# One-hot marks of places moved from VectorE to ScalarE in six edge passes of a graph network

## Chip, cores and metric
One core of a Trainium2 chip runs the whole program in one launch. The metric is device time in microseconds, from the start to the end of the execution; lower is better.

## What is computed
Four graph layers run one after the other over 6250 nodes with 256 features and 100000 edges, each followed by a residual and a layer norm:

```
x = layernorm(x + L0(x)); x = layernorm(x + L1(x)); x = layernorm(x + L2(x)); x = layernorm(x + L3(x))
# L0: two GAT layers, 4 heads of 64 and 1 head of 64
alpha = segment_softmax(leaky_relu(al_s[src] + al_d[dst]), dst)
out   = segment_sum(h[src] * alpha, dst)
# L1: two heads of 128
e   = exp(-leaky_relu(s_l[src] + s_r[dst]))
out = elu(segment_sum(e * h[dst], src) / segment_sum(e, src))
# L2: 8 heads of 32
s   = sum(q[row] * k[col])
out = segment_sum(segment_softmax(s, row) * v[col], row)
# L3: two graph convolutions, 128 and 64 wide, with batch norm
out = segment_sum(h[src] * dinv[src] * dinv[dst], dst)
```

In each of these the edges gather a row of a table of nodes and are summed by their target node. That makes six passes over the edges: a1e and a2e (L0), be (L1), te (L2), g1e and g2e (L3).

## The kernel before
The edges are first sorted twice, by source and by target. After that every node window of 128 nodes has its edges in groups of 128 slots; 832 groups (NSLOT) make 104 batches (NBT) of 8 groups. Of each slot `order.row` holds the row to gather, `order.place` the place of its target node in the window (0 to 127, larger for an empty slot), and `order.window` the group's window. The tables and sums stay in float32.

A pass goes over the 104 batches, written out in full (`batches`), each engine with its own `step`, tied by semaphores:

- POOL (`gather`, L948 and L1325) issues 8 indirect DMAs a batch. It waits for DVE's copy of the index of the batch and for the ring of row buffers to be free: in the attention passes until DVE has weighed the batch that lay there (`s_summand`), in the sum passes until PE has summed it. The ring holds 4 batches, in te 2.
- DVE `mark` (L1109 to L1113, L1354 to L1358) makes `onehot`: for 8 groups of 128 slots a 128x1024 float32 tile that is 1 where the lane number equals the slot's place. There are two buffers, so it waits for PE's sums of the batch before last.
- DVE `weigh` multiplies the gathered rows by their weights into `summand`, two groups at a time, `add` adds PE's result of a group to its window in `acc`, with a window number held in a register. The registers are loaded for a few batches at a time (`Windows.load`).
- PE `sums` (L987) multiplies `onehot` by `summand`, one matmul a group into one of four PSUM banks; `add` must have freed the bank. In the sum passes (L1339) PE takes the gathered rows as they are, and has eight banks.
- In the passes with a guarded softmax (a1e, a2e, te) there is a running maximum besides: PE `flat` turns the logits, DVE `scan_forward` and `scan_back` scan them, PE `ends` brings the edges of the scan to one row, DVE scans that row (`row_scan_forward`, `row_scan_back`, `drop`), PE `columns` (L1012) spreads it again, using row 0 of `onehot`, DVE `widen` and `top` finish the maximum, PE `back` turns it back and DVE `subtract` makes the argument of the exponent.
- ACT does little: `fading` (L1083) takes the exponential that PE's `columns` makes ready, with which DVE `fade_first` scales an open window; `weights` (L1075) takes the exponentials of the arguments into `summand`. In be it has only `weights`; in the sum passes there is no ACT block.

The order of DVE's work in a batch is written out in `step` (L1231 and L1364). There the mark stands behind the last adds of the batch before last and in front of the third weighing and the forward scan; in the sum passes it is the first thing of a step. PE's order is in L1029: flat, sums 2 and 3, ends, sums 4 and 5, columns, sum 6, back, sum 7, with small differences between the passes.

Of the kernel before, what the change touches and what calls it, by code (L numbers as in the profile page):

```python
# [13 lines left out]
P = 128  # L14
# [49 lines left out]
def bc(ap, shape):  # L64
    return ap.to_broadcast(shape)
# [767 lines left out]
def attention_pass(nc, c, stage, order, tables, table, width, acc, Y, H, C, kind, node=None, value_c0=0, queries=None, early=None):  # L833
# [21 lines left out]
    with ExitStack() as stack:  # L855
# [5 lines left out]
        place_row = [m.sb(f"place_row{b}", [P, 8 * P], F16) for b in range(2)]  # L861
        turned = [m.sb(f"turned{b}", [P, 8 * P], F32 if dot else BF16) for b in range(2)]
        onehot = [m.sb(f"onehot{b}", [P, 8, P]) for b in range(2)]
        argument = [m.sb(f"argument{b}", [P, NARG, H, 8]) for b in range(2)]
        ps_u = [m.ps(f"ps_u{b}", [P, 512]) for b in range(4)]
        if dot:
# [6 lines left out]
        if guarded:  # L873
# [15 lines left out]
        s_flags = [m.sem(f"flags{b}") for b in range(2)]  # L889
        (s_index, s_turned, s_onehot, s_at_node, s_spread, s_raw, s_logit, s_joined, s_product, s_query, s_weight, s_summand, s_summed, s_added,  # L890
         s_flat, s_forward, s_local, s_ends, s_row_forward, s_row_peak, s_fall, s_columns, s_fade, s_widened, s_peak, s_back, s_argument, s_own,
         s_faded, s_ready, s_early, s_passed, s_passed_pe, s_passed_sp, s_passed_act) = (m.sem(x) for x in (
            "index", "turned", "onehot", "at_node", "spread", "raw", "logit", "joined", "product", "query", "weight", "summand", "summed", "added",
            "flat", "forward", "local", "ends", "row_forward", "row_peak", "fall", "columns", "fade", "widened", "peak", "back", "argument", "own",
            "faded", "ready", "early", "passed", "passed_pe", "passed_sp", "passed_act"))

        def lives(t):
            return not isinstance(t, int) or 0 <= t < NBT
# [8 lines left out]
        def batches(eng, step, last=NBT, windows=None):  # L907


            for t in range(last):  # L910
                if windows is not None and t % U == 0:
                    windows.load(t)
                step(t, t % U)

        with nc.Block() as block:
# [157 lines left out]
            @block.scalar  # L1073
            def _(act):
                def weights(t, b):  # L1075
                    act.wait_ge(s_argument, t + 1)
                    wait(act, s_summed, t * 8 - 8)
                    out = summand[:, b, :, :].rearrange("p k (h n) -> p h k n", h=H)
                    act.activation(out[:, :, :, C], argument[b][:, 0, :, :], ACT.Exp, scale=1.0 if guarded else -1.0).then_inc(s_weight, 1)
                    if gat:  # L1080
                        act.activation(out[:, :, :, C + 1], argument[b][:, 1, :, :], ACT.Exp).then_inc(s_weight, 1)

                def fading(t, b):  # L1083
                    act.wait_ge(s_columns, t + 1)
                    wait(act, s_faded, t - 1)
                    act.activation(fade[b][:, :], ps_l[:, 256:256 + H], ACT.Exp).then_inc(s_fade, 1)

                def step(t, j):
                    if guarded:
                        fading(t, j % 2)  # L1090
                    weights(t, j % 2)

                batches(act, step)

            @block.vector
            def _(dve):
# [6 lines left out]
                def turn(t, b):  # L1103
                    if lives(t):
                        dve.wait_ge(s_place[b], t * 8 + (16 - b * 8))
                        wait(dve, s_query if dot else s_at_node, t * 4 - 4 if dot else t - 1)
                        dve.tensor_scalar(turned[b][:, :], place_row[b][:, :], c.lane_p[:, :], None, ALU.is_equal).then_inc(s_turned, 1)  # L1107

                def mark(t, b):  # L1109
                    if lives(t):  # L1110
                        wait(dve, s_summed, t * 8 - 8)
                        dve.tensor_tensor(onehot[b][:, :, :], bc(c.lane[:, :].rearrange("p (k n) -> p k n", k=1), [P, 8, P]),
                                          bc(order.place[:, bass.ds(t * 8, 8)].rearrange("p (k n) -> p k n", n=1), [P, 8, P]), ALU.is_equal).then_inc(s_onehot, 1)  # L1113

                def weigh(t, b, r, pair):
                    if not lives(t):
# [114 lines left out]
                def step(t, j):  # L1231
# [18 lines left out]
                    else:  # L1250
# [8 lines left out]
                        if gat:  # L1259
                            join(t, b)  # L1260
                        add(t - 2, 7, -9, j)
                    mark(t, b)
                    weigh(t - 1, n, rp, 2)
                    if guarded:
                        scan_forward(t, b)
# [33 lines left out]
def sum_pass(nc, c, stage, order, table, width, acc):  # L1299
# [4 lines left out]
    with ExitStack() as stack:  # L1304
        m = Memory(nc, stack, stage)
        rows = m.sb("rows", [P, RING, 8, width])
        index = m.sb("index", [P, RING, 8], I32)
        onehot = [m.sb(f"onehot{b}", [P, 8, P]) for b in range(2)]
        ps_u = [m.ps(f"ps_u{b}", [P, 512]) for b in range(8)]
        s_rows = [[m.sem(f"rows{r}_{h}") for h in range(2)] for r in range(RING)]  # L1310
        s_index, s_onehot, s_summed, s_added, s_passed = (m.sem(x) for x in ("index", "onehot", "summed", "added", "passed"))

        def lives(t):
            return not isinstance(t, int) or 0 <= t < NBT
# [7 lines left out]
        with nc.Block() as block:  # L1322
# [15 lines left out]
            def _(pe):  # L1338
# [8 lines left out]

                batches(pe, step)

            @block.vector  # L1350
            def _(dve):
                windows = Windows(nc, order, mybir.EngineType.DVE, -8, RING)

                def mark(t, b):  # L1354
                    if lives(t):
                        wait(dve, s_summed, t * 8 - 8)
                        dve.tensor_tensor(onehot[b][:, :, :], bc(c.lane[:, :].rearrange("p (k n) -> p k n", k=1), [P, 8, P]),
                                          bc(order.place[:, bass.ds(t * 8, 8)].rearrange("p (k n) -> p k n", n=1), [P, 8, P]), ALU.is_equal).then_inc(s_onehot, 1)  # L1358
# [553 lines left out]
```

## Time and profile before

| | us |
|---|---|
| median of 3 runs | 13213.7 (13208.91 to 13229.04) |
| profiled execution | 13124.58 |
| its span, first to last instruction | 13122.8 |
| DVE busy | 8087.8 (62%) |
| PE busy | 7310.8 (56%) |
| POOL busy | 5296.6 (40%) |
| ACT busy | 580.3 (4%) |

The profile is of one execution. "Busy" is the time in which an engine works on an instruction; waits, register and issue instructions are not in it. A line such as L1112 is a line of the kernel. In a row with a bracket, the bracket tells how long the engine was idle before the instruction and what ended the wait; "issue" is a wait for nothing that the profile shows, "remote" one whose releaser it can't tell. PEld is the load of weights into TensorE. The sorting takes the first 2700 us or so, and holds none of the changed code.

### The profile page before, as it was taken

The page shows a single profiled execution, that of the slowest core. Times are in us where ns is not written, and L with a number is a line of the kernel's source. Part 1 is how long each engine was busy: PE and PEld are TensorE (multiplying, and loading weights), DVE is VectorE, ACT ScalarE, POOL GpSimd, SP SyncE. Part 2 cuts the span into 40 slices and gives each one's busy share as a digit, 9 for nine tenths or more (in the row PEclk, how much of TensorE's full clock was granted, in tenths as well). Part 3 has the DMA queues.
Part 4 walks back from the last instruction along what each step waited for, and adds up shares of the span by engine and source line. Part 5 has one row for each costly group of instructions (what it writes and reads, how often), then busy time and mean ns, then how long its engine had stood idle before and what let it go on. Part 6 is the DMA issues. An engine that isn't in the chain of part 4 may idle for free. (4 is left out here: it accounts for less than half of the span.)

```text
span 13122.8 us, 152037 instructions
## 1 busy us (share of the span) xinstructions
PE 7310.8 (56%) x32826; PEld 4771.1 (36%) x32826; DVE 8087.8 (62%) x27204; ACT 580.3 (4%) x2200; POOL 5296.6 (40%) x5059
## 2 busy tenths in 40 slices
PE   4555355568886455556665466666666433333335
PEld 2333233344444344433333234444443323223333
DVE  9999899957777444445665666666664322332224
ACT  0000000010001000001000100000001000000001
POOL 0000000046662566615777033333330666556670
PEclk6777677765655555557666776666665555555557
DMA  0111111133332221213444133333330111211111
GB/s 18 50 50 51 38 50 50 53 93 107 106 106 53 60 43 42 42 10 105 114 111 110 64 113 112 112 112 111 111 102 31 45 45 45 38 20 23 23 23 22
DMA packets 456540, 857.24 MB, mean 65 GB/s; under 512 B 136865, under 2 KB 197974, under 8 KB 455766
## 3 DMA queue, kind: packets, MB, share of 16 engines
q0 software_dynamic: 226304, 550.69, 17.4%
q1 hardware_dynamic: 229718, 300.70, 7.8%
q8 instruction: 196, 3.21, 0.1%
q14 instruction: 322, 2.64, 0.1%
HBM read 798.81 MB, written 52.14 MB: 65 GB/s over the span
## 5 line engine op out<-in xcount | busy, mean ns | idle before, releaser
L954 POOL DMA_INDIRECT all_Y<-table,te_index x832 | 851.1, 1023 | 1384.9 <-DVE all_Y L1123 1177.1
L954 POOL DMA_INDIRECT all_Y<-table,a1e_index x832 | 891.3, 1071 | 454.6 <-issue 245.4
L954 POOL DMA_INDIRECT all_Y<-table,be_index x832 | 942.0, 1132 | 292.9 <-issue 245.8
L954 POOL DMA_INDIRECT all_Y<-table,a2e_index x832 | 833.0, 1001 | 515.5 <-DVE all_Y L1123 293.1
L1330 POOL DMA_INDIRECT g2e_rows<-table,g2e_index x832 | 839.6, 1009 | 447.1 <-issue 247.8
L1330 POOL DMA_INDIRECT g1e_rows<-table,g1e_index x832 | 815.4, 980 | 481.5 <-issue 236.0
L994 PE MATMUL te_ps_u<-all_Y,te_onehot 128*128 128x264 f32 x1664 | 749.1, 566 | 458.1 <-DVE all_Y L1123 384.2
L1123 DVE TENSOR_TENSOR all_Y<-all_Y 128x512 f32<-128x512 f32 (+1 forms) x1664 | 964.6, 580 | 40.3 <-issue 18.1
L994 PE MATMUL be_ps_u<-all_Y,be_onehot 128*128 128x258 f32 x1664 | 722.7, 572 | 430.0 <-DVE all_acc L1135 257.5
L994 PE MATMUL a1e_ps_u<-all_Y,a1e_onehot 128*128 128x264 f32 x1664 | 878.8, 654 | 83.8 <-DVE all_acc L1135 47.2
L1346 PE MATMUL g1e_ps_u<-g1e_rows,g1e_onehot 128*128 128x128 f32 x1664 | 485.1, 444 | 757.8 <-issue 478.3
L1346 PE MATMUL g2e_ps_u<-g2e_rows,g2e_onehot 128*128 128x64 f32 x1664 | 426.0, 429 | 798.4 <-issue 412.6
L940 POOL MEMSET all_acc<- 128x13200 f32 (+2 forms) x4 | 35.9, 8973 | 1903.0 <-POOLq L80 1794.4
L1371 DVE TENSOR_TENSOR all_acc<-all_acc,g1e_ps_u 128x128 f32 x832 | 239.4, 288 | 828.7 <-DMA te_turns<-turns_src 501.6
L1371 DVE TENSOR_TENSOR all_acc<-all_acc,g2e_ps_u 128x64 f32 x832 | 184.0, 221 | 862.6 <-DMA te_turns<-turns_src 414.5
L1346 PEld LDWEIGHTS g1e_ps_u<-g1e_rows,g1e_onehot 128*128 128x128 f32 x1664 | 378.6, 291 | 864.2 <-issue 658.9
L493 DVE TENSOR_SCALAR all_acc<-all_Y,all_acc 128x832 f16<-128x832 f16 x1568 | 687.4, 438 | 0.0
L1346 PEld LDWEIGHTS g2e_ps_u<-g2e_rows,g2e_onehot 128*128 128x128 f32 x1664 | 377.1, 324 | 847.3 <-issue 555.1
L994 PEld LDWEIGHTS be_ps_u<-all_Y,be_onehot 128*128 128x128 f32 x1664 | 383.0, 267 | 711.9 <-issue 500.2
L994 PEld LDWEIGHTS te_ps_u<-all_Y,te_onehot 128*128 128x128 f32 x1664 | 372.9, 257 | 668.1 <-DVE all_Y L1123 627.7
L983 PE MATMUL te_ps_q<-all_X,te_turned 128*128 x1664 | 570.7, 503 | 23.2 <-DVE te_turned L1107 22.1
L994 PE MATMUL a2e_ps_u<-all_Y,a2e_onehot 128*128 128x66 f32 x1664 | 498.8, 429 | 90.6 <-DVE all_acc L1135 69.8
(464 smaller groups left out, 15600.2 us busy)
## 6 DMA issues: line engine op xcount, KB each, us to landing
all_Y<-lows SPq DMA_DIRECT2D x196, 256.0 KB
all_Y<-codes SPq DMA_DIRECT2D x196, 256.0 KB
a1e_place_row<-places_dst SPq DMA_DIRECT2D x104, 256.0 KB
a2e_place_row<-places_dst SPq DMA_DIRECT2D x104, 256.0 KB
be_place_row<-places_src SPq DMA_DIRECT2D x104, 256.0 KB
te_place_row<-places_src SPq DMA_DIRECT2D x104, 256.0 KB
all_Y<-table,a1e_index POOLq DMA_INDIRECT x832
all_Y<-table,a2e_index POOLq DMA_INDIRECT x832
```

What stands on the lines that cost most here:

```text
L493: dve.tensor_scalar(column1[b][:, k, :], lane16, column[b][:, k:k + 1], None, ALU.is_equal)
L940: pool.memset(acc[:, 0:NW * R], 0.0).then_inc(s_ready, 1)
L954: pool.indirect_dma_start(out=rows[:, r, k, :], out_offset=None, in_=table, in_offset=bass.IndirectOffsetOnAxis(ap=index[:, r, k:k + 1], a ...
L983: last = pe.matmul(ps_q[pair % 2][:, j * HC:(j + 1) * HC], turned[b][:, k * P:(k + 1) * P], queries[:, bass.ds(windows.at(windows_j, chunk ...
L994: pe.matmul(ps_u[k % 4][:, 0:R], onehot[b][:, k, :], summand[:, b, k, :], start=True, stop=True).then_inc(s_summed, 1)
L1123: dve.tensor_tensor(out[:, :, :, 0:C], rows[:, r, ks, value_c0:value_c0 + HC].rearrange("p k (h n) -> p k h n", h=H), bc(out[:, :, :, C:C ...
L1330: pool.indirect_dma_start(out=rows[:, r, k, :], out_offset=None, in_=table, in_offset=bass.IndirectOffsetOnAxis(ap=index[:, r, k:k + 1], a ...
L1346: pe.matmul(ps_u[k][:, 0:width], onehot[b][:, k, :], rows[:, r, k, :], start=True, stop=True).then_inc(s_summed, 1)
L1371: dve.tensor_tensor(mine, mine, ps_u[k][:, 0:width], ALU.add).then_inc(s_added, 1)
```

## The change
ScalarE makes `onehot` in all six passes. Places and lane numbers are whole numbers, so 1 - |place - lane|, cut at zero, is 1 where they agree and 0 elsewhere. ScalarE takes the distance of each of the 8 groups in an ACTIVATE of its own (Abs, with the place as the bias of a partition) into a float16 tile, then Relu of one minus the distance for the 8 at once. In the attention passes `mark(0, 0)` comes first, and the mark of batch t+1 behind the weights of batch t; in the sum passes ScalarE gets a block that makes one mark after the other. DVE's `mark` goes in both functions. One tile `distance` is added, and one semaphore.

```diff
@@ attention_pass
+        distance = m.sb("distance", [P, 8, P], F16)
...
             @block.scalar
...
+                def mark(t, b):
+                    if lives(t):
+                        wait(act, s_onehot, t)
+                        for k in range(8):
+                            act.activation(distance[:, k, :], c.lane[:, :], ACT.Abs, scale=-1.0, bias=order.place[:, t * 8 + k:t * 8 + k + 1]).then_inc(s_distance, 1)
+                        act.wait_ge(s_distance, t * 8 + 8)
+                        wait(act, s_summed, t * 8 - 8)
+                        act.activation(onehot[b][:, :, :], distance[:, :, :], ACT.Relu, scale=-1.0, bias=1.0).then_inc(s_onehot, 1)
...
                     weights(t, j % 2)
-
+                    mark(t + 1, 1 - j % 2)
+
+                mark(0, 0)
                 batches(act, step)
...
             @block.vector
...
-                def mark(t, b):
-                    if lives(t):
-                        wait(dve, s_summed, t * 8 - 8)
-                        dve.tensor_tensor(onehot[b][:, :, :], bc(c.lane[:, :].rearrange("p (k n) -> p k n", k=1), [P, 8, P]),
-                                          bc(order.place[:, bass.ds(t * 8, 8)].rearrange("p (k n) -> p k n", n=1), [P, 8, P]), ALU.is_equal).then_inc(s_onehot, 1)
...
-                    mark(t, b)
                     weigh(t - 1, n, rp, 2)
@@ sum_pass
+            @block.scalar
+            def _(act):
+                def mark(t, b):
...
+                for t in range(NBT):
+                    mark(t, t % 2)
+
             @block.vector
...
-                    mark(t, r % 2)
                     for k in range(8):
```

The `mark` of the sum passes' ScalarE block is the same five lines as above, and DVE's `mark` (L1354) goes there as it does in the attention passes.

## Rows read from the trace of the kernel before

**Rows 1.** The page, part 1: busy time of each engine, share, instructions.
```profile
PE 7310.8 (56%) x32826; PEld 4771.1 (36%) x32826; DVE 8087.8 (62%) x27204; ACT 580.3 (4%) x2200; POOL 5296.6 (40%) x5059
```

**Rows 2.** Stretches: us, then PE, PEld, DVE, ACT, POOL busy (count), PEclk, DMA share, GB/s.
```profile
2760.00:4110.00 1350.00, 1085.07 (x3884) 642.38 (x3885) 1039.16 (x2964) 56.73 (x308) 871.41 (x813) 0.59 0.41 104
...
6020.00:7240.00 1220.00, 766.59 (x2416) 437.64 (x2416) 751.94 (x1813) 23.43 (x101) 928.38 (x819) 0.66 0.43 111
7600.00:9820.00 2220.00, 1469.07 (x4701) 953.69 (x4701) 1511.66 (x3269) 51.04 (x206) 835.41 (x816) 0.69 0.40 111
10205.00:11420.00 1215.00, 478.81 (x1640) 373.14 (x1640) 355.55 (x1018) 0.00 (x0) 804.10 (x823) 0.54 0.19 45
11605.00:12790.00 1185.00, 417.40 (x1630) 369.15 (x1629) 301.79 (x1018) 0.00 (x0) 824.49 (x819) 0.50 0.14 23
```

**Rows 3.** Groups by form, DVE: the mark in te; the other five alike, 126.7 to 127.1.
```profile
L1112 DVE TENSOR_TENSOR te_onehot<-all_lane,all_place 128x1024 f32<-128x1024 f32 x104 | 126.7, 1218 | 0.1
```

**Rows 4.** The page, part 5: gathers of a1e, be, g2e, g1e; busy, mean ns, idle.
```profile
L954 POOL DMA_INDIRECT all_Y<-table,a1e_index x832 | 891.3, 1071 | 454.6 <-issue 245.4
L954 POOL DMA_INDIRECT all_Y<-table,be_index x832 | 942.0, 1132 | 292.9 <-issue 245.8
...
L1330 POOL DMA_INDIRECT g2e_rows<-table,g2e_index x832 | 839.6, 1009 | 447.1 <-issue 247.8
L1330 POOL DMA_INDIRECT g1e_rows<-table,g1e_index x832 | 815.4, 980 | 481.5 <-issue 236.0
```

**Rows 5.** Timeline of te around one mark: start, duration, engine, line.
```profile
7914.59 0.27 PE L1001 MATMUL te_ps_l<-all_ident,te_joined 128*72 128x128 f32 x1
7915.03 1.22 DVE L1112 TENSOR_TENSOR te_onehot<-all_lane,all_place 128x1024 f32<-128x1024 f32 x1
...
7916.16 0.69 DVE L1123 TENSOR_TENSOR all_Y<-all_Y 128x512 f32<-128x512 f32 x1
...
7918.16 0.64 PE L1009 MATMUL te_ps_r<-all_ident,te_local 72*1 72x72 f32 x4 [3.30 <-DVE te_local L1193]
```

**Rows 6.** Timeline of a1e: PE's sums 2 and 3 and its ends matmul.
```profile
3407.98 2.08 PE L994 MATMUL a1e_ps_u<-all_Y,a1e_onehot 128*128 128x264 f32 x4
...
3411.04 0.29 PE L1009 MATMUL a1e_ps_r<-all_ident,a1e_local 36*1 36x36 f32 x4 [0.98 <-DVE a1e_local L1193]
```

**Rows 7.** Waits in the stretches of rows 2 (a2e: 4330 to 5650): us, times, longest.
```profile
DVE a2e_forward L1188 <- remote: 324.9, 47, 9.4
...
DVE a1e_forward L1188 <- remote: 23.7, 1, 23.7
...
POOL g1e_rows L1330 <- PE g1e_ps_u L1346: 172.7, 79, 8.6
```

**Rows 8.** Timeline of be: two gathers on POOL, then DVE's mark beside the second.
```profile
6512.32 0.95 POOL L954 DMA_INDIRECT all_Y<-table,be_index  x1 [0.30 <-issue]
6513.57 1.57 POOL L954 DMA_INDIRECT all_Y<-table,be_index  x1 [0.30 <-issue]
...
6513.10 1.22 DVE L1112 TENSOR_TENSOR be_onehot<-all_lane,all_place 128x1024 f32<-128x1024 f32 x1
```

**Rows 9.** Timeline of g1e: a late and a quick add on DVE, POOL's gather after standstill.
```profile
10747.32 0.29 DVE L1371 TENSOR_TENSOR all_acc<-all_acc,g1e_ps_u 128x128 f32 x1 [5.31 <-DMA te_turns<-turns_src]
...
10752.53 0.29 DVE L1371 TENSOR_TENSOR all_acc<-all_acc,g1e_ps_u 128x128 f32 x1 [0.21 <-DVE all_acc L1371]
...
10751.40 1.04 POOL L1330 DMA_INDIRECT g1e_rows<-table,g1e_index  x1 [5.12 <-PE g1e_ps_u L1346]
```

**Rows 10.** ACT: four ACTIVATEs in a row; one group; the table load; a1e's fading.
```profile
12900.11 0.76 ACT L734 ACTIVATE gfl_turned<-gfl_ps_t 128x128 f32<-128x128 f32 x4 [2.45 <-PE gfl_ps_t L697]
...
L1589 ACT ACTIVATE a1l_tile<-a1l_ps_o 128x264 f32<-128x264 f32 x50 | 19.6, 391 | 28.8 <-PE a1l_ps_o L708 28.8
...
L237 ACT ACT_TABLE_LOAD x1 | 1.3, 1283 | 4.8 <-PEq L109 4.8
...
3414.40 0.17 ACT L1086 ACTIVATE a1e_fade<-a1e_ps_l 128x4 f32<-128x4 f32 x1 [9.76 <-PE a1e_ps_l L1019]
```

More of the change, by code:

```diff
@@ L891, in attention_pass @@
          s_flat, s_forward, s_local, s_ends, s_row_forward, s_row_peak, s_fall, s_columns, s_fade, s_widened, s_peak, s_back, s_argument, s_own,
-         s_faded, s_ready, s_early, s_passed, s_passed_pe, s_passed_sp, s_passed_act) = (m.sem(x) for x in (
+         s_faded, s_ready, s_early, s_distance, s_passed, s_passed_pe, s_passed_sp, s_passed_act) = (m.sem(x) for x in (
             "index", "turned", "onehot", "at_node", "spread", "raw", "logit", "joined", "product", "query", "weight", "summand", "summed", "added",
             "flat", "forward", "local", "ends", "row_forward", "row_peak", "fall", "columns", "fade", "widened", "peak", "back", "argument", "own",
-            "faded", "ready", "early", "passed", "passed_pe", "passed_sp", "passed_act"))
+            "faded", "ready", "early", "distance", "passed", "passed_pe", "passed_sp", "passed_act"))
         def lives(t):
@@ L1308, in sum_pass @@
         onehot = [m.sb(f"onehot{b}", [P, 8, P]) for b in range(2)]
+        distance = m.sb("distance", [P, 8, P], F16)
         ps_u = [m.ps(f"ps_u{b}", [P, 512]) for b in range(8)]
         s_rows = [[m.sem(f"rows{r}_{h}") for h in range(2)] for r in range(RING)]
-        s_index, s_onehot, s_summed, s_added, s_passed = (m.sem(x) for x in ("index", "onehot", "summed", "added", "passed"))
+        s_index, s_onehot, s_summed, s_added, s_distance, s_passed = (m.sem(x) for x in ("index", "onehot", "summed", "added", "distance", "passed"))
         def lives(t):
@@ L1348, in _ @@
                 batches(pe, step)
+            @block.scalar
+            def _(act):
+                def mark(t, b):
+                    if lives(t):
+                        wait(act, s_onehot, t)
+                        for k in range(8):
+                            act.activation(distance[:, k, :], c.lane[:, :], ACT.Abs, scale=-1.0, bias=order.place[:, t * 8 + k:t * 8 + k + 1]).then_inc(s_distance, 1)
+                        act.wait_ge(s_distance, t * 8 + 8)
+                        wait(act, s_summed, t * 8 - 8)
+                        act.activation(onehot[b][:, :, :], distance[:, :, :], ACT.Relu, scale=-1.0, bias=1.0).then_inc(s_onehot, 1)
+                for t in range(NBT):
+                    mark(t, t % 2)
             @block.vector
@@ L1352, in _ @@
                 windows = Windows(nc, order, mybir.EngineType.DVE, -8, RING)
[L1354 to L1358, printed above, removed]
                 def stage_index(t, r):
```

## The prediction, made before the changed kernel ran
> **What bounds the kernel now.** I read the page's busy shares first: no engine is full over the span, DVE 62%, PE 56%, POOL 40%, ACT 4% [rows 1]. So the stages have different limits, and the change touches six of them. The table of stretches gives each pass's middle: te 2220 us, a1e 1350, be 1220, g1e 1215, g2e 1185 [rows 2]; a2e is near a1e. ACT works 0 to 57 us in any of them, so it has room everywhere; what matters is whether DVE's 1.22 us mark [rows 3] lies on the path of each pass.
>
> - te: 2220 us for 816 gathers, that is 102 batches, 21.8 us each. DVE is busy 1512 us and idle only where PE or ACT answers it; POOL is busy 835 us [rows 2]. The timeline shows the mark between the turn and the weighing with no gap on either side [rows 5]. DVE sets the pace.
> - a1e: 1350 us, DVE 1039, POOL 871 [rows 2]. DVE is in one long chain with PE. POOL's gathers with their 0.3 us of issue between them need less: 891 busy + 245 of issue = 1137 us of some 1380 [rows 4].
> - a2e: 47 batches lose time in front of the forward scan, 324.9 us together, to a "remote" releaser; in a1e that happens once, 23.7 us [rows 7].
> - be: POOL is the limit. 942 us busy, and of its 292.9 us of idle 245.8 are issue, which leaves 47 for any wait [rows 4].
> - g1e and g2e: POOL runs 804 and 824 us in 1215 and 1185 [rows 2]; with issue 1054 and 1071. The rest, 161 and 114 us, is POOL waiting; in g1e 172.7 us are put down to PE's sums [rows 7]. DVE is busy for only 356 and 302 us, yet it is what POOL finally waits for: the adds stand 0.2 us apart at one time and over 5 us apart at another [rows 9]. The releaser named there is a DMA of a finished pass, so the true cause of the long gaps is not in the view. They appear while POOL gathers without a pause and end when POOL has stood still for 5 us. Some queue seems to fill under gap-free gathers, and PE's results reach DVE late. I take this as a limit that the mark does not touch.
>
> **The change, part by part.** Removed: 104 marks on DVE in each pass. On DVE a mark costs from its start to the next one's start: 7915.03 to 7916.16, 1.13 us [rows 5]; times 104 is 118 us a pass, 705 in six, if all of it were on the path.
>
> Added on ACT, per batch: eight distances of 128x128 and one Relu of 128x1024. Four ACTIVATEs of 128x128 took 0.76 us together, one alone 0.27 [rows 10]: 0.16 us each once they follow one another, so eight take 0.27 + 7 x 0.16 = 1.4 us (2.2 if nothing overlaps). The Relu: 264 elements took 0.391 us [rows 10], against 128 in 0.27 that is 0.85 to 0.9 ns an element, so 1024 take 1.05 us. A mark on ACT is 2.5 us, at most 3.3, against 11.5 to 22 us a batch. I cost it at nothing; its cover is ACT's idleness. Its order: behind the weights of batch t stands the mark of t+1, and behind that the fading of t+1. In a1e ACT stood idle 9.76 us between the weights and the fading [rows 10], room for 2.5. The mark's own wait is for the last sum of t-1, which PE issues around then; the mark is first needed by PE's columns, just before the fading. In be the next thing queued is the weights a batch later, in the sum passes nothing. There ACT has to keep up with DVE's quick step, eight adds 0.5 us apart and an index copy, 4.2 us [rows 9]; 2.5 to 3.3 does.
>
> The table of functions: the one load of the whole trace took 1.28 us and serves Exp, Copy and Square [rows 10]. No row shows Abs or Relu. From below it is nothing. From above two loads a batch, 2.6 us, still fit into ACT's gap, so I take nothing. The Trainium skill (ScalarE: Activation LUTs, Table sets) says that relu and abs are in every set; no run here shows it. Its rules for authors say to keep relu on VectorE since it is faster there per element; by that the work would be dearer, and the rows say that it is dearer on an engine that has nothing else to do.
>
> The port. A gather on POOL takes 0.95 us alone and 1.57 when a mark runs on DVE beside it [rows 8]. Over a pass the gathers spend more than 832 x 0.95 = 790 us by 101 in a1e, 152 in be, 25 in g1e, 49 in g2e [rows 4]. The mark's share is between nothing (the weighing next to it stretches gathers too) and 0.6 us x 104 = 64 us in be, and all of it in g1e and g2e. The Trainium skill (SBUF — State Buffer, Who interferes with whom) says that a tensor_tensor with two SBUF inputs contends only with POOL's reads and did not stall descriptor generation. By that rule the relief would be nil and be would gain at most its 47 us. The trace shows the stretching, so I count relief, but only part.
>
> Now the passes.
> - te: flat's transpose has ended at 7914.86, before the mark does, so the scan behind the weighing needn't wait, and PE's ends stand 3.3 us waiting for DVE's local [rows 5]. All of it, but for rounding: 117.
> - a1e: PE's four passes of sums end at 3410.06 and its ends matmul started at 3411.04 [rows 6], so 0.98 of 1.13 gets through at most where the clock is slow: 102 to 118 (104 batches). Bound from below 0, if late answers of PE come here too. I take 95.
> - a2e: where DVE waits at the scan the mark is hidden. That leaves 57 of 104 batches, x 1.13 = 64; more bursts may bring more waits. Bounds 0 and 118; I take 45.
> - be: 47 of waiting plus 64 of stretching are the upper end, 111; 0 the lower. POOL issues on either way; I take 45, nearer to the wait than to the sum.
> - g1e: the upper end is the mark, 118 (POOL has 177 + 25 to give); the lower 0, if the late answers set the pace. I take 35, somewhat over the port's 25.
> - g2e: 118 and 0 likewise, POOL having 115 + 49; 35.
>
> Sum: 117 + 95 + 45 + 45 + 35 + 35 = 372 us. The profiled execution took 13124.6 us, so it would take 12753. The median of the runs is 13213.7, 0.7% above the profiled one, though the runs lie within 0.15%; I take the gain off the median: 12842, say 12840. About 0.2% is what a measurement of this kernel can tell from no change.
>
> **Rivals.**
> A. Full release: the marks are on the path in all DVE-driven passes, and the long gaps in g1e and g2e shrink with DVE's load. Then te 118, a1e 118, a2e 64, be 111, g1e 118, g2e 118 = 647, and 12567. For it: in g1e's quick stretches an add comes every 0.5 us [rows 9], eight in 4.0, so the mark is a fifth of DVE's step. Against: the over-5 us gaps, which hold no DVE work. Chance 0.20.
> B. Gathers bind: be, g1e and g2e average 1.49, 1.48 and 1.45 us a gather (stretch over POOL's count) [rows 2], where an undisturbed one needs 1.25; if the unseen queue sets that average, all three give 15 together, a2e 15, te 117 and a1e 95: 242, and 12972. Chance 0.15.
> C. Slower: in a1e DVE's slowness gives POOL a pause each batch, and a1e has one remote wait before the forward scan where a2e has 47 [rows 7]. If the freed DVE makes gathers in a1e gap-free, that wait comes there too, at 324.9 / 47 = 6.9 us. The other passes gain 277, so it decides from 277 / 6.9 = 40 of 104 batches on. With 60 batches: 414 - 277 = 137 more, 13351. Against: a1e takes 13.3 us a batch now (813 gathers, 8 a batch), 12.2 after the change, and POOL needs 11.0 [rows 2], which leaves a pause, and POOL's standstill ends such a phase. Chance 0.07.
> D. No change: the time shows up again as waits for PE in every pass, since PE is also near its limit in te and a1e at a low clock. The idle PE before ends [rows 5] speaks against it. 13214, chance 0.04.
>
> **How the numbers follow.** The forecast has the other 0.54, and spans gains of 270 to 500. The range runs from 12610, most of the way to A, to 13000, past B: outside are C, D and the far part of A, under 2 in 10. Faster: forecast, A and B, 0.89. Same: 0.04. Slower: 0.07.
>
> **What the changed profile would show.** No onehot write on DVE in the passes and DVE busy down by about 760 us; on ACT 4992 distances near 0.27 us and 624 Relus near 1.05, so ACT up by some 2000 us of counted time, with one table load. te's middle near 2105 us. In te the forward scan follows weigh 2 without a gap: a gap there says that flat is late. The gathers near 0.95 us where marks stretched them. Wrong would be: more remote waits before a1e's scan (C), the fading waiting for ACT rather than PE's columns, more than two table loads, or g1e and g2e shorter by over 100 us each (A).

## The result: 0.7% slower, and the profile after

Ten timed runs each: 13290.65 us (13235.81 to 13305.5) with the change, 13211.89 (13123.92 to 13247.68) before; ratio 1.0067, 95% interval 1.0043 to 1.0091. The forecast was 12840, between 12610 and 13000. The profiled execution of after took 13302.03 us, that of before 13124.58, which is one of the quick ones of its kernel (two of the ten timed runs lie there too): the two profiles differ by 177 us, the medians by 79. The sum below is made between the profiles.

The page of after, part 1, as in [rows 1]:
```profile
PE 7158.1 (54%) x32826; PEld 4698.6 (35%) x32826; DVE 7399.3 (56%) x26580; ACT 2706.2 (20%) x7816; POOL 5028.2 (38%) x5059
```
The page of after, part 5, the gathers, as in [rows 4] (busy, mean ns of one | idle, what ended most of it):
```profile
L955 POOL DMA_INDIRECT all_Y<-table,te_index x832 | 852.7, 1025 | 1257.7 <-DVE all_Y L1129 1047.6
L955 POOL DMA_INDIRECT all_Y<-table,a1e_index x832 | 846.9, 1018 | 623.2 <-DVE all_Y L1129 397.3
L955 POOL DMA_INDIRECT all_Y<-table,a2e_index x832 | 801.3, 963 | 607.9 <-DVE all_Y L1129 370.9
L955 POOL DMA_INDIRECT all_Y<-table,be_index x832 | 830.0, 998 | 462.8 <-issue 239.9
L1336 POOL DMA_INDIRECT g2e_rows<-table,g2e_index x832 | 786.6, 945 | 530.8 <-issue 258.8
L1336 POOL DMA_INDIRECT g1e_rows<-table,g1e_index x832 | 786.6, 945 | 529.0 <-issue 262.4
```
In the attention passes busy and idle together are the time from the first gather to the last: in be 942.0 + 292.9 = 1235 before and 830.0 + 462.8 = 1293 after. The change made POOL 112 us shorter there and idle 170 us longer. In a1e it is busy 44 less and idle 169 more. In the sum passes the idle time also holds some 68 and 82 us ahead of the first gather. From the first gather to the last, us:

| | a1e | a2e | be | te | g1e | g2e |
|---|---|---|---|---|---|---|
| before | 1345 | 1347 | 1232 | 2235 | 1228 | 1203 |
| after | 1469 | 1408 | 1291 | 2109 | 1247 | 1234 |
| difference | +124 | +61 | +59 | -126 | +19 | +31 |

These make +168 of the 177. So te gained what was forecast, and the other five lost. Waits of DVE in after, in a1e, a2e and be (us, times, longest), as in [rows 7]:
```profile
DVE a1e_forward L1194 <- remote: 178.2, 29, 13.4
...
DVE a1e_widened L1219 <- remote: 80.8, 21, 11.8
...
DVE a1e_row_forward L1204 <- remote: 29.5, 8, 6.3
...
DVE a2e_widened L1219 <- remote: 388.1, 81, 6.8
...
DVE all_acc L1141 <- remote: 411.6, 88, 14.5
```
The same three kinds in a1e were 28.5 us before: a forward scan of 23.7, a widening of 4.8. In a2e the remote waits of DVE grew as well, from 431 us to 590 together; most stood before the forward scan (327.3 us) and now stand before the widening. The waits named remote stand in front of a different operation in each line, but each of these waits for a semaphore that PE raises: flat, columns, ends, sums. In be the wait before the adds was 139.3 us, 33 times, and is now 411.6 us, 88 times.

The timeline of after, g1e, shows what such a wait is, as in [rows 9] (start, duration, engine, line, in brackets the idle time and its releaser):
```profile
10800.27 0.29 DVE L1384 TENSOR_TENSOR all_acc<-all_acc,g1e_ps_u 128x128 f32 x1 [4.34 <-issue]
...
10801.58 0.95 POOL L1336 DMA_INDIRECT g1e_rows<-table,g1e_index  x1 [0.30 <-issue]
10802.83 0.94 POOL L1336 DMA_INDIRECT g1e_rows<-table,g1e_index  x1 [0.30 <-issue]
10804.08 0.95 POOL L1336 DMA_INDIRECT g1e_rows<-table,g1e_index  x1 [0.30 <-issue]
10805.19 0.29 DVE L1384 TENSOR_TENSOR all_acc<-all_acc,g1e_ps_u 128x128 f32 x1 [4.64 <-issue]
...
10805.53 0.80 PE L1352 MATMUL g1e_ps_u<-g1e_rows,g1e_onehot 128*128 128x128 f32 x2 [4.07 <-issue]
...
10810.32 0.95 POOL L1336 DMA_INDIRECT g1e_rows<-table,g1e_index  x1 [0.31 <-issue]
...
10814.95 1.06 ACT L1365 ACTIVATE g1e_onehot<-g1e_distance 128x1024 f32<-128x1024 f16 x1 [24.04 <-DMA te_turns<-turns_src]
10815.00 0.29 DVE L1384 TENSOR_TENSOR all_acc<-all_acc,g1e_ps_u 128x128 f32 x1 [3.91 <-DMA te_turns<-turns_src]
...
10816.27 0.94 POOL L1336 DMA_INDIRECT g1e_rows<-table,g1e_index  x1 [5.00 <-PE g1e_ps_u L1352]
10817.38 0.29 DVE L1384 TENSOR_TENSOR all_acc<-all_acc,g1e_ps_u 128x128 f32 x1 [2.01 <-issue]
...
10817.88 0.29 DVE L1384 TENSOR_TENSOR all_acc<-all_acc,g1e_ps_u 128x128 f32 x1 [0.21 <-DVE all_acc L1384]
10818.38 0.29 DVE L1384 TENSOR_TENSOR all_acc<-all_acc,g1e_ps_u 128x128 f32 x1 [0.21 <-DVE all_acc L1384]
```
Read it by the code. PE has eight banks, so the matmul at 10805.53 is the one that waited for the add at 10805.19 to free its bank; the seven sums ahead of it stand in the trace as done long ago (counted off, the add at 10810.80 takes one that started at 10788.6). The answer from DVE to PE is quick: the matmul starts 0.34 us after the add's start, 0.05 after its end. The answer from PE to DVE is late, and ACT's Relu, which waits for the same count of the same semaphore as the add at 10815.00, starts with it. Two engines see it at one time, so what is late is not the engine that waits. It lasts while POOL gathers every 1.25 us; when POOL has stood still for 5 us, the adds follow each other every 0.50 us. I call these the late answers. The profile's end of a matmul is modelled. The Trainium skill (Perfetto Trace Analysis, Tensor Engine Instruction) says the same, and that the update goes out only after PSUM has acknowledged the write.

Whether the sum or its update was late can't be told from the ends of the matmuls, but the trace also holds the times of the semaphores' updates (625 for the sums of 816 matmuls of this pass; the others are missing in it). Seven of them stand between 10815.62 and 10815.87, 0.04 us apart, while POOL stands still; no two recorded sums of this pass end less than 0.22 us apart. So these sums were done, and their updates were held back and came together. An update of DVE or ACT in this pass comes within 0.02 us of its instruction's end. Of PE's, 261 of the 625 come over 1.5 us behind the last recorded matmul that could have sent them.

### The profile page after: what moved, and what is told of

Read it like the earlier page. It is cut to its first block and busy times, and to the rows that moved or that the text cites. A ratio compares the mean times of both kernels' runs of the same rounds, so it can differ in the third digit from the quotient of the medians.

```text
span 13300.3 us, 157641 instructions
## 1 busy us (share of the span) xinstructions
PE 7158.1 (54%) x32826; PEld 4698.6 (35%) x32826; DVE 7399.3 (56%) x26580; ACT 2706.2 (20%) x7816; POOL 5028.2 (38%) x5059
## 5 line engine op out<-in xcount | busy, mean ns | idle before, releaser
L955 POOL DMA_INDIRECT all_Y<-table,a1e_index x832 | 846.9, 1018 | 623.2 <-DVE all_Y L1129 397.3
L955 POOL DMA_INDIRECT all_Y<-table,a2e_index x832 | 801.3, 963 | 607.9 <-DVE all_Y L1129 370.9
L955 POOL DMA_INDIRECT all_Y<-table,be_index x832 | 830.0, 998 | 462.8 <-issue 239.9
L1336 POOL DMA_INDIRECT g2e_rows<-table,g2e_index x832 | 786.6, 945 | 530.8 <-issue 258.8
L1336 POOL DMA_INDIRECT g1e_rows<-table,g1e_index x832 | 786.6, 945 | 529.0 <-issue 262.4
L995 PE MATMUL be_ps_u<-all_Y,be_onehot 128*128 128x258 f32 x1664 | 663.3, 533 | 535.8 <-issue 278.1
L995 PE MATMUL te_ps_u<-all_Y,te_onehot 128*128 128x264 f32 x1664 | 695.0, 529 | 473.3 <-DVE all_Y L1129 399.2
L493 DVE TENSOR_SCALAR all_acc<-all_Y,all_acc 128x832 f16<-128x832 f16 x1568 | 727.5, 464 | 0.0
L1141 DVE TENSOR_TENSOR all_acc<-all_acc,be_ps_u 128x258 f32 x832 | 349.7, 420 | 608.5 <-remote 411.6
L995 PEld LDWEIGHTS te_ps_u<-all_Y,te_onehot 128*128 128x128 f32 x1664 | 345.2, 240 | 664.8 <-DVE all_Y L1129 597.7
```

Source lines behind the costliest of these rows:

```text
L493: dve.tensor_scalar(column1[b][:, k, :], lane16, column[b][:, k:k + 1], None, ALU.is_equal)
L955: pool.indirect_dma_start(out=rows[:, r, k, :], out_offset=None, in_=table, in_offset=bass.IndirectOffsetOnAxis(ap=index[:, r, k:k + 1], a ...
L995: pe.matmul(ps_u[k % 4][:, 0:R], onehot[b][:, k, :], summand[:, b, k, :], start=True, stop=True).then_inc(s_summed, 1)
L1141: dve.tensor_tensor(mine, mine, ps_u[k % 4][:, 0:R], ALU.add).then_inc(s_added, 1)
L1336: pool.indirect_dma_start(out=rows[:, r, k, :], out_offset=None, in_=table, in_offset=bass.IndirectOffsetOnAxis(ap=index[:, r, k:k + 1], a ...
```

## The experiments

Theory L: the freed DVE and the unstretched gathers give POOL more stretches without a pause, and in these PE's answers come late. Theory S: ScalarE's own work costs. The runs were made on five chips (e1 to e4, e5 to e8, e9 to e12, e13 to e16, e17 and e18), each with the kernel before beside it. A difference of some 20 us in a pass between runs of two chips can be the chips'. Times of the runs and, from the first gather to the last, of the passes, us:

| run | before, same chip | median | ratio (95%) | a1e | a2e | be | te | g1e | g2e |
|---|---|---|---|---|---|---|---|---|---|
| e1 te only | 13127 | 13003 | 0.9909 (0.9893 to 0.9926) | 1338 | 1347 | 1233 | 2112 | 1227 | 1205 |
| e2 both | 13127 | 13056 | 0.9944 (0.9928 to 0.9961) | 1344 | 1381 | 1241 | 2116 | 1244 | 1214 |
| e3 nobody | 13127 | 13086 | 0.9965 (0.9951 to 0.9979) | 1390 | 1361 | 1258 | 2113 | 1223 | 1222 |
| e4 pause 1 | 13127 | 13135 | 1.0022 (1.0000 to 1.0044) | 1415 | 1386 | 1261 | 2114 | 1214 | 1210 |
| e5 pause 128 | 13194 | 13171 | 0.9992 (0.9965 to 1.0018) | 1449 | 1391 | 1250 | 2113 | 1232 | 1229 |
| e6 te only, pause 128 | 13194 | 12998 | 0.9870 (0.9827 to 0.9914) | 1340 | 1347 | 1244 | 2112 | 1216 | 1210 |
| e7 one increment | 13194 | 13284 | 1.0066 (1.0028 to 1.0104) | 1459 | 1402 | 1294 | 2112 | 1252 | 1241 |
| e8 pause 256 | 13194 | 12886 | 0.9783 (0.9739 to 0.9826) | 1312 | 1328 | 1242 | 2112 | 1200 | 1200 |
| e9 before, pause 256 | 12557 | 13084 | 1.0419 (1.0402 to 1.0437) | 1324 | 1254 | 1277 | 2236 | 1250 | 1232 |
| e10 nobody, pause 256 | 12557 | 12759 | 1.0161 (1.0144 to 1.0178) | 1292 | 1226 | 1247 | 2110 | 1201 | 1201 |
| e11 pause a batch | 12557 | 12692 | 1.0108 (1.0091 to 1.0125) | 1288 | 1205 | 1240 | 2109 | 1179 | 1179 |
| e12 pause 384, 224 | 12557 | 12845 | 1.0230 (1.0213 to 1.0248) | 1372 | 1318 | 1205 | 2108 | 1178 | 1178 |
| e13 changed | 13193 | 13263 | 1.0059 (1.0041 to 1.0076) | 1455 | 1404 | 1294 | 2109 | 1240 | 1234 |
| e14 before | 13193 | 13113, one run | | 1368 | 1366 | 1244 | 2232 | 1234 | 1207 |
| e15 before, pause 256 | 13193 | 13114 | 0.9944 (0.9919 to 0.9969) | 1323 | 1276 | 1278 | 2234 | 1254 | 1236 |
| e16 nobody, pause 256 | 13193 | 12864, one run | | 1292 | 1296 | 1241 | 2116 | 1200 | 1200 |
| e17 pause a batch | 12558 | 12706 | 1.0098 (1.0067 to 1.0129) | 1289 | 1208 | 1242 | 2112 | 1179 | 1180 |
| e18 pause by pass | 12558 | 12750 | 1.0153 (1.0136 to 1.0170) | 1291 | 1281 | 1207 | 2111 | 1180 | 1180 |

### Where the loss comes from

**e1.** ScalarE marks in te alone.
```diff
-                    mark(t + 1, 1 - j % 2)
+                    if dot:
+                        mark(t + 1, 1 - j % 2)
```
(DVE keeps its `mark` in the other five.)

> Theory L (late answers): PE's increments of its semaphores reach DVE and ACT late while POOL gathers every 1.25 us without a pause, and the freed DVE gives POOL more of such stretches; te has none, since DVE sets its pace. Theory S (ScalarE): the marks on ScalarE themselves, their traffic and their nine semaphore increments a batch, hold up the other engines. Here ScalarE marks in te alone. L: te falls from 2235 us (first to last gather) to about 2109, as in the changed kernel, the other five stay at the values of before (1345, 1347, 1232, 1228, 1203), so the kernel is 110 to 130 us faster than before, a ratio near 0.990. S says the same of the other five, and of te nothing else; this run only shows that the parts add up.

As expected: te 2112, the others as before, and the kernel is 0.9% faster than before.

**e2.** The changed kernel, and DVE compares too, at the old place, into a tile of its own (not in te).
```diff
+                    if not dot:
+                        compare(t, b)
                     weigh(t - 1, n, rp, 2)
```

> The changed kernel, with VectorE making its comparison too in a1e, a2e, be, g1e and g2e, at the old place, into a tile that nothing reads. L: DVE's pace and the stretched gathers are back, so the five passes go back to the times of before within 20 us each (1345, 1347, 1232, 1228, 1203 against 1469, 1408, 1291, 1247, 1234), te stays at 2109: near 13000 on the profile, 1 per cent faster than before. S: the marks of ScalarE still cost, and the compare comes on top: the five stay at the changed kernel's times or above them, the whole at 13300 or more.

a1e 1344 and be 1241 are back at before's times, with ScalarE marking as in the changed kernel. g2e (1214) is back for the greater part, a2e (1381) is still 34 above before, and g1e (1244) stays near the changed kernel's 1247. Giving DVE its 118 us of work back makes a1e some 120 us shorter. L holds for a1e and be; a part of a2e's loss and nearly all of g1e's do not go. DVE's waits in a1e in this run:
```profile
DVE a1e_forward L1202 <- remote: 23.5, 2, 23.3
DVE a1e_widened L1227 <- remote: 9.9, 2, 6.2
```

**e3.** No marks behind the first two batches; the tiles hold ones, so the places are left out of the sums.
```diff
-                    mark(t + 1, 1 - j % 2)
+                    if t == 0:
+                        mark(t + 1, 1 - j % 2)
```

> No engine makes marks behind the first two batches: both tiles hold ones from then on (the places are left out of the sums). L: it is as slow as the changed kernel or slower, a1e over 1430, a2e over 1390, be over 1270, g1e and g2e over 1235, since DVE is freed and POOL's gathers are not stretched. S: with ScalarE's work gone the five passes fall under the values of before, each by up to 118 us, the whole to 12600 to 12800.

Neither theory had it right alone. The five passes take 6454 us together, where e1 on the same chip has 6350: to take DVE's marks away, with ScalarE making none either, costs 104 us. What ScalarE's marks add to that is less sure, since the changed kernel did not run on this chip. On two others its five passes take 293 us more than those of the kernel before (6649 and 6356) and 208 more (e13 and e14, 6627 and 6419), so the marks would add 104 to 189. With DVE's comparison in place they add 74 (e2, 6424), and e4 below, the changed kernel on this chip with a very short memset on POOL, takes only 32 more than e3 (6486).

**e7.** One increment behind the eighth distance in place of eight.
```diff
-                        act.wait_ge(s_distance, t * 8 + 8)
+                        act.wait_ge(s_distance, t + 1)
```

> The changed kernel, whose eight distances raise their semaphore once, behind the eighth, in place of eight times. Without marks the five passes took 1390, 1361, 1258, 1223, 1222 against 1469, 1408, 1291, 1247, 1234: 195 us are ScalarE's. If these come from the number of increments, the time falls by most of 195: the profile near 13120 to 13180. If they come from ScalarE's work itself (its reads and writes, or the later mark), it stays at 13280 to 13300 on the first chip's scale, some 150 above the short pause.

13284 where the kernel before has 13194, the changed kernel's own ratio again. The number of increments is not ScalarE's cost.

The times of the semaphores' updates show the late answers themselves. Of PE's recorded updates in each pass, the share that comes over 1.5 us behind the last recorded matmul that could have sent it (of PE's updates up to a third are missing in these traces, and three fifths in g1e of e8):

| % | a1e | a2e | be | te | g1e | g2e |
|---|---|---|---|---|---|---|
| before | 1 | 32 | 11 | 0 | 33 | 28 |
| after | 22 | 23 | 32 | 0 | 42 | 36 |
| e2 both | 1 | 28 | 6 | 0 | 40 | 35 |
| e3 nobody | 13 | 31 | 27 | 0 | 27 | 46 |
| e8 pause 256 | 8 | 36 | 10 | 0 | 12 | 36 |

In a1e and be it is high where the loss is, and te has none. In a2e it falls with the change, though the waits grow; that is not explained.

### A pause on POOL

**e4, e5, e8.** The changed kernel with a memset on POOL behind each gather, of 1, 128 and 256 elements a partition, in all passes but te.
```diff
                         ).then_inc(s_rows[r][k // 4], 16)
+                        wait(pool, s_paused, (t * 8 + k) // 1)
+                        pool.memset(pause[:, :], 0.0).then_inc(s_paused, 1)
```

> The changed kernel, with a memset of one element a partition on POOL behind each gather in five passes (not in te): 0.10 us and its issue, so a gather takes 1.35 to 1.45 us in place of 1.25. L: the late answers become rare. be, g1e and g2e go to 832 x 1.40 = 1165 to 1200 us, a1e under 1345, a2e under 1300: the whole 12750 to 12950. S, or any theory in which POOL is just short of time: the passes stay or get longer, up to 832 x 0.15 = 125 us each where POOL sets the pace, the whole at 13300 or more.

> As the run with the short pause, but the memset has 128 elements a partition (0.21 us in place of 0.10), so that gathers inside a burst come every 1.40 to 1.45 us in place of 1.31. L: fewer late answers again; be, g1e and g2e 1180 to 1210 us (832 x 1.42 = 1181 is what POOL itself needs), a1e 1340 to 1390, a2e 1340 to 1370, the whole 12950 to 13080. If POOL's time were what counts, the five passes would be 832 x 0.1 = 83 us longer each than with the short pause, near 13500.

> The same again with 256 elements, about 0.33 us: gathers every 1.5 to 1.55 us. L with POOL's own need on top: be, g1e and g2e 832 x 1.53 = 1273 us, now set by POOL; a1e and a2e with hardly a remote wait, a1e 1290 to 1340, a2e 1310 to 1350. It tells whether the late answers go altogether when gathers are spaced, or whether a1e keeps them.

More work for POOL makes the kernel faster: e8 takes 3.0% less than e7 on the same chip. e4 and e5 gained far less than was expected of them (13135 for 12750 to 12950, 13171 for 12950 to 13080). Where nothing holds POOL up, gathers of g1e come every 1.25 us without a pause and 1.25 with 1 element too, since that memset fits into the 0.30 us of issue (the expectation of e5 took 1.31 for it); they come every 1.33 with 128 and 1.44 with 256. So e4 was hardly a test of a slower pace. The answers are still late at 1.33, one add each 4 to 5 us, as in e5:
```profile
10604.58 0.29 DVE L1393 TENSOR_TENSOR all_acc<-all_acc,g1e_ps_u 128x128 f32 x1 [3.16 <-DMA te_turns<-turns_src]
...
10609.50 0.29 DVE L1393 TENSOR_TENSOR all_acc<-all_acc,g1e_ps_u 128x128 f32 x1 [4.64 <-DMA te_turns<-turns_src]
```
At 1.44 no gather of be, g1e or g2e starts over 2.5 us behind the one before it (54, 35 and 36 do in the changed kernel), and g1e takes 1200 us in place of 1247. The expectation of e8 for be, g1e and g2e (1273) was wrong since the memset takes up half of the 0.30 us of issue. In the timeline of e8, g1e, POOL alone:
```profile
10500.66 0.33 POOL L1348 MEMSET g1e_pause<- 128x256 f32 x1
10501.15 0.95 POOL L1343 DMA_INDIRECT g1e_rows<-table,g1e_index  x1 [0.17 <-issue]
10502.09 0.33 POOL L1348 MEMSET g1e_pause<- 128x256 f32 x1
10502.58 0.95 POOL L1343 DMA_INDIRECT g1e_rows<-table,g1e_index  x1 [0.16 <-issue]
```
And DVE there: four adds together, as half a batch lands, no late one among these:
```profile
10507.43 0.29 DVE L1393 TENSOR_TENSOR all_acc<-all_acc,g1e_ps_u 128x128 f32 x1 [3.81 <-PE g1e_ps_u L1361]
10507.93 0.29 DVE L1393 TENSOR_TENSOR all_acc<-all_acc,g1e_ps_u 128x128 f32 x1 [0.21 <-issue]
10508.42 0.29 DVE L1393 TENSOR_TENSOR all_acc<-all_acc,g1e_ps_u 128x128 f32 x1 [0.21 <-issue]
10508.92 0.29 DVE L1393 TENSOR_TENSOR all_acc<-all_acc,g1e_ps_u 128x128 f32 x1 [0.21 <-issue]
```
Late answers are left even so. In g2e as large a share of updates is late as in the changed kernel, but no add that waits for one stands for over 2.7 us, and POOL's pace, 832 times 1.44 us, sets the pass's time. In a2e the waits stay long, which is why it stays at 1328:
```profile
DVE a2e_forward L1199 <- remote: 230.2, 46, 10.4
```
The memset shows one thing more: it waits for nothing but POOL's own memset before it, and in e4, in g1e, even that count comes late. The wait is put down to a DMA of long ago:
```profile
10369.25 0.10 POOL L1348 MEMSET g1e_pause<- 128x1 f32 x1 [1.59 <-DMA g_W<-in_L_gnn_W]
```
Of the 236 updates of it that the trace holds in g1e, 129 come over 0.5 us behind the memset's end, the latest 3.4 us; in e5 44 of 182; in e8 none of 445. So POOL's updates are held back as well as PE's, while DVE's and ACT's come within 0.06 us in a1e, be, g1e and g2e of these runs.

**e6.** The pause of 128 elements in e1's kernel.

> ScalarE marks in te alone, VectorE elsewhere, and the same pause of 128 elements in the other five passes. L: g1e and g2e gain from the pause also without the change, 1180 to 1200 us against 1227 and 1205; be and a1e had few late answers and POOL's stretched gathers already, so there the pause brings nothing or costs: be 832 x 1.6 = 1300 at most, a1e 1340. If the pause helps only where ScalarE marks, g1e and g2e stay at 1227 and 1205 or get longer.

Against e1, on another chip, g1e gains 11 us, be and g2e lose 11 and 5; 1180 to 1200 were expected of g1e and g2e. With DVE's mark in place a short pause mends little.

### The other kernels with the pause, and another chip

**e9 to e12** have the pause of 256 elements in the kernel before and in e3's kernel, one memset a batch (1856 elements, 1664 in the sum passes), and 384 elements in a1e and a2e with 224 in be, g1e and g2e. The edit of e11, in the sum passes, and of e12:
```diff
+                        if k % 8 == 7:
+                            wait(pool, s_paused, (t * 8 + k) // 8)
+                            pool.memset(pause[:, :], 0.0).then_inc(s_paused, 1)
...
+        pause = None if dot else m.sb("pause", [P, 384 if gat else 224])
```

> The kernel before, with the pause of 256 elements in the five passes (not te), where the changed kernel with it took 1312, 1328, 1242, 2112, 1200, 1200 us. L: spaced gathers have no late answers in either kernel, and then the mark costs what it did by its own time where DVE sets the pace. g1e and g2e 1200 to 1240 (POOL's 832 x 1.444, and the mark's stretch), be 832 x 1.52 = 1265 to 1310, a1e 1345 to 1380, te 2235; the whole 13050 to 13200. So with the pause in both kernels the change is worth 150 to 300 us, where without it it costs 80 to 170. If the pause alone makes e8's gain, the five passes come out as in the changed kernel with the pause, within 15 us each.

> No marks behind the first two batches (places left out of the sums), with the pause of 256 elements. Without the pause ScalarE's marks cost 195 us in the five passes. If that cost came through the late answers too, it goes with them: each pass within 15 us of the changed kernel with this pause (1312, 1328, 1242, 1200, 1200). If ScalarE's work costs on its own, this run is again 100 us or more faster in the five.

> The changed kernel with one long memset on POOL a batch (1856 elements, about 1.6 us, in the attention passes but te, 1664 in the sum passes), so that POOL gathers 8 times at 1.25 us and then pauses: 1.42 to 1.44 us a gather on the mean, as the pause of 256 elements gives. If the mean rate counts, the passes come out as there, 1190 to 1250 for be, g1e, g2e. If the gathers must be spaced one by one, the late answers stay: g1e and g2e over 1225, a1e over 1400.

> The changed kernel with 384 elements in a1e and a2e (about 0.44 us, 1.55 us a gather, 1290 us a pass) and 224 in be, g1e and g2e (0.30 us, 1.41 us a gather, 1173 us). L: a1e 1290 to 1310, a2e 1290 to 1320, be 1200 to 1240, g1e and g2e 1173 to 1190 if 1.41 is still slow enough to keep the answers in time; over 1200 if not. The whole 12800 to 12900.

The chip of these four was another sort: the kernel before takes 12557 us on it, not 13127 to 13213, and all four are slower than it. No answer is late there: each of PE's updates in the six passes comes within 0.02 us of a matmul's end, and so it is in e17 and e18. With the pause a2e has no late answer left; DVE waits for the gathers instead, in e9:
```profile
DVE a2e_raw L1159 <- DMA all_Y<-table,a2e_index: 323.0, 100, 5.5
```
So the four say little of L, save that a chip can be without late answers, at least under a pause; e12 says that 384 elements are too many (a1e 1372).

**e13 to e16** are the changed kernel, the kernel before, and e9 and e10 again.

> The changed kernel as it is, to see it on another chip. Where the kernel before takes about 13130 to 13210 us (a chip with late answers): 13220 to 13300, some 0.6 per cent slower. Where the kernel before takes about 12560 (a chip without): the change gains, te 126, a1e 60 to 120, and in be, g1e and g2e what the gathers are no longer stretched (up to 150, 25, 50), 12100 to 12350 us, 1.5 to 3.5 per cent faster.

> The kernel before, with a profile on the same chip as the run above. On a chip with late answers the passes are those shown of before (1345, 1347, 1232, 2235, 1228, 1203). On a chip without, g1e and g2e take 832 x 1.28 to 1.32 = 1065 to 1100 us and hold no add that waits over 3 us while POOL gathers, be is about 1200, a2e 1150 or less, te the same 2235.

> The kernel before with the pause of 256 elements in the five passes. On a chip with late answers: near 13050 to 13130, since the spaced gathers keep the answers in time but the marks still cost DVE's time; the changed kernel with the same pause took 12886, so with the pause the change is worth 150 to 250. On a chip without: 13084 as measured, the pause being pure loss.

> No marks behind the first two batches, with the pause of 256 elements. On a chip with late answers the changed kernel with this pause took 1312, 1328, 1242, 2112, 1200, 1200. If ScalarE's cost came through the late answers, be, g1e, g2e are the same within 15 us and a1e and a2e up to 30 less; if it is a cost of its own, each pass is 20 or more shorter. On a chip without: 12762 as measured.

This chip has late answers again. The pair repeats the result (1.0059). With the pause in both kernels the change is worth 13114 - 12886 = 228 us (e15 and e8, on two chips whose kernel before takes 13193 and 13194): te 122, g1e 54, g2e 36, be 36, a1e 11, and a2e loses 52; that is 207 of it. Without marks at all (e16) be, g1e and g2e take the same 1241, 1200, 1200 as with ScalarE's: at this pace of POOL its work costs nothing there. That fits a cost that came through the late answers, but does not show it, since a cost below POOL's pace would be hidden. a1e and a2e are 20 and 32 us shorter in e16; whether that is a cost of ScalarE's own is open, since both still have some remote waits in e8. The gathers of be show the comparison's stretch, on DVE (e15) and with no mark (e16):
```profile
L956 POOL DMA_INDIRECT all_Y<-table,be_index x832 | 860.1, 1034 | 147.3 <-issue 142.7
```
```profile
L957 POOL DMA_INDIRECT all_Y<-table,be_index x832 | 817.0, 982 | 147.3 <-issue 142.9 <-DVE all_Y L1135 3.6 <-DVE be_index L1119 0.9
```

**e17, e18.** The pause a batch again, and a version by pass: 256 elements in a1e, 320 in a2e, 224 in be, g1e and g2e.
```diff
+        pause = None if dot else m.sb("pause", [P, (320 if H == 1 else 256) if gat else 224])
```

> The changed kernel with one long pause a batch, 8 gathers at 1.25 us and then 2.6 to 2.8 us of gap, 1.42 to 1.44 us a gather on the mean. On the chip without late answers it took 1288, 1205, 1240, 2109, 1179, 1179. If the mean rate decides, the same within 25 us each on a chip with late answers, except a2e (1205 to 1330, as with 256 elements): the whole 12690 to 12850. If the gathers must be apart one by one, g1e and g2e are over 1225, a1e over 1400, the whole over 13100.

> Pause of 256 elements in a1e, 320 in a2e, 224 in be, g1e and g2e, ScalarE marks everywhere. On a chip with late answers: a1e 1312, a2e 1270 to 1300, be 1205 to 1220, te 2110, g1e and g2e 1178, the whole 12740 to 12800, some 3 per cent faster than the kernel before. If 1.42 us a gather is too quick for that chip, g1e and g2e are over 1200 and hold adds that wait over 3 us.

The chip was again one on which before takes 12558. e18 beats e12 by 95 us on such a chip and loses 1.5% to the kernel before; e17 repeats e11. Whether the mean pace of the gathers decides or each one's distance, for which the two were made, stays open: neither ran on a chip with late answers, so e8 is the fastest version measured on one: 2.2% under the kernel before (0.9739 to 0.9826), 2.8% under the changed kernel by the two ratios.

## Why the prediction was wrong

- **te** was right: 117 forecast, 126 measured. The forward scan follows the weighing without a gap. The granted clock in the pass was 0.75 (0.69 before, [rows 2]), which may be the rest. The row of te's stretch in after, columns as in [rows 2]:
```profile
7825.00:9955.00 2130.00, 1427.92 (x4768) 939.06 (x4768) 1415.37 (x3206) 394.58 (x1135) 850.43 (x830) 0.75 0.42 118
```
- **ACT's price** was mis-sized. Eight distances take 2.44 us, where 1.4 (at most 2.2) was forecast from four in a row at 0.76; the Relu takes 1.06 against 1.05. The mark is 3.5 us, over the "at most 3.3", and still hidden as far as its own time goes: in g1e PE waited 12.8 us for it in the whole pass. "I cost it at nothing" failed another way. By the comparisons under e3 ScalarE's marks are a part of the loss, 32 to 189 us in the five passes, in a way that no run shows. The Trainium skill (VectorE: DVE Perf Modes, The TRN2 errata) gives ScalarE 224 cycles and one per element at 1.2 GHz; by that an estimate is 2.35 us for the eight, and the trace agrees better with it than with mine.
```profile
L1088 ACT ACTIVATE be_distance<-all_lane,all_place 128x128 f16<-128x128 f32 x832 | 253.1, 386 | 12.0 <-PEq L1526 12.0
...
L1091 ACT ACTIVATE be_onehot<-be_distance 128x1024 f32<-128x1024 f16 x104 | 109.9, 1057 | 863.3 <-PE be_ps_u L995 644.3 <-remote 201.4 <-issue 17.6
```
- **The table of functions** cost nothing: one load in the trace, 1.28 us, as before.
- **The port** was right as a mechanism: the gathers of be fell from 1132 to 998 ns on the mean, those of g1e and g2e to 945 each, and e15 against e16 shows it with nothing else changed. The Trainium skill (SBUF — State Buffer, Who interferes with whom) says that a tensor_tensor with both inputs in SBUF contends with GpSimd's reads, with which this agrees, and that it was not seen to stall descriptor generation, which does not hold for these gathers. But the relief was counted as gain. POOL used it to come sooner to the end of what the late answers allow.
- **The step that failed** is "I take this as a limit that the mark does not touch". The late answers were seen in g1e and g2e, named as a queue that fills under gathers without a pause, and then held constant, while the same sum took away what made the pauses: DVE's 1.13 us a batch and the stretched gathers. With that limit moving, and ScalarE's marks adding to it, the 95, 45, 45, 35 and 35 us of a1e, a2e, be, g1e and g2e became -124, -61, -59, -19 and -31. The share of PE's late updates rose from 1 to 22% in a1e and from 11 to 32% in be.
- **Rival C** had the mechanism and a chance of 0.07. It confined it to a1e and priced 60 waits of 6.9 us. Measured in a1e: 29 remote waits before the forward scan of 6.1 us each, 21 before the widening, 8 before the row's scan, 288 us together; and be, g1e, g2e and a2e lost too. The argument against it failed too: POOL has its pauses in a1e (184 waits for DVE's weighing, 397 us), and they did not keep the answers in time.
- **Rival B** (the unseen queue sets the average) came with a gain of 15 us in three passes. That a queue which sets the pace could get worse when it is fed faster was in no case.
- **The profile's forecasts**: DVE busy fell by 688, not 760 (the six marks are 761; the sort's small operations, which the change doesn't touch, were some 0.03 us longer each in this execution). ACT rose by 2126 with 5616 more instructions, as said.

Still open: what in the chip holds the updates of PE and POOL back, why some chips do not (12557 against 13127 to 13213), what the unpaused changed kernel takes on such a chip, and how ScalarE's marks add to the loss once DVE's are gone. The tracing may have a part in it: on the two quick chips the traces hold all of PE's updates in the passes, on the others some are missing, in some passes over half. No run tells whether the updates are late without tracing. On a chip without them, e1's and e8's gains were not measured.

## What to carry to other kernels

Where an engine or a link gets slower the faster it is fed, freeing time elsewhere can cost more than it gives: before counting a relief as gain, ask which unexplained wait it feeds. A wait that the profile calls remote, or puts down to a transfer of a finished pass, is best read through the code, for the engine that raises the semaphore; when it comes and goes with another engine's bursts, a short pause in those bursts tests it in one run. A gain in one pass and a loss in the others can be taken apart: e1 keeps the gain of te for 0.9%.

## What the chip showed that was not expected

- In the changed kernel adds of g1e started up to 34 us behind the recorded end of their matmul while POOL issued a gather every 1.25 us, and in the stretch shown they stood 4.2 to 5.6 us apart. At 1.44 us a gather the waits were short in be, g1e and g2e (4.8, 2.6 and 2.7 us at the longest), at 1.33 they were not.
- What is late is the semaphore's update: seven of PE's came within 0.26 us, 0.04 us apart, when POOL stood still. POOL's own updates were up to 3.4 us late in g1e of e4. DVE's and ACT's came within 0.02 us of the end in g1e.
- On two of the five chips of the experiments the kernel before took 12557 and 12558 us, 4 to 5% less than on the others, and the kernels with a pause had none of these waits there. The same pause is +4.2% on such a chip (e9) and -0.6% on another (e15).
